# Row maxima of attention scores turned two slots at a time, a turned context kept in memory, routing in groups of six over three rounds

## The reference

```python
x = x + L0_xattn(ctx, ctx, layernorm(x))       # A: one head; keys and values from ctx
x = x + L0_ffn(layernorm(x))                   # B: 32 heads of width 8, then a GELU FFN, one expert a batch
x = x + L1_xattn(layernorm(x), ctx)            # C: one head over ctx, and a self score per token
x = x + L1_ffn(layernorm(x))                   # D: 16 heads of width 16, then a routed FFN
```

## Time and profile before

| | us |
|---|---|
| three timed runs | 2184.40, 2190.86, 2193.01 (median 2190.86) |
| the profiled execution | 2177.86 |
| its span in the profile | 2175.9 |
| TensorE, VectorE, ScalarE, GpSimd busy | 1970.9, 1389.9, 1040.9, 588.0 |

### The profile page before, as it was taken

One profiled execution on the slowest core, in us unless ns is written; L12 is line 12 of the kernel. 1 busy time (PEld: TensorE's weight loads), 2 busy tenths in 40 slices (PEclk: granted clock), 3 DMA queues, 4 the chain that ended last, 5 costly groups with the idle time before them and its releaser, 6 DMA issues. The chain is left out here.

```text
span 2175.9 us, 38554 instructions
## 1 busy us (share of the span) xinstructions
PE 1970.9 (91%) x13917; PEld 1466.8 (67%) x13917; DVE 1389.9 (64%) x3655; ACT 1040.9 (48%) x2001; POOL 588.0 (27%) x476
## 2 busy tenths in 40 slices
PE   4689999999999999999999999999977649999996
PEld 3456666676766666666767666666655428999996
DVE  2336666666766667666766667666677546767663
ACT  1244655565665555565665555564632214333331
POOL 1102031312213121212213131211200136667773
PEclk9679999999999999999999999999988769999998
DMA  5221433514142332414142342414120243344232
GB/s 176 78 73 53 144 112 98 170 67 155 57 146 80 127 129 100 159 58 155 61 145 87 117 144 100 151 42 151 56 69 1 78 144 98 84 123 88 44 53 25
DMA packets 197003, 217.45 MB, mean 100 GB/s; under 512 B 13656, under 2 KB 186544, under 8 KB 196816
## 3 DMA queue, kind: packets, MB, share of 16 engines
q1 hardware_dynamic: 182432, 198.01, 27.4%
q0 software_dynamic: 14384, 16.99, 4.8%
HBM read 146.63 MB, written 68.32 MB: 99 GB/s over the span
## 5 line engine op out<-in xcount | busy, mean ns | idle before, releaser
L1170 DVE TENSOR_REDUCE MX<-bank 128x2 f32<-128x512 f32 x768 | 493.0, 683 | 212.2 <-PE bank L826 211.0
L1408 ACT ACTIVATE PT<-bank 128x512 f32<-128x512 f32 x768 | 416.7, 596 | 233.4 <-PE bank L863 231.6
L826 PE MATMUL bank<-KS,QS 32*128 32x256 f32 (+1 forms) x1536 | 199.4, 338 | 34.9 <-DVE MX L1170 30.0
L878 PE MATMUL bank<-PT,VA 128*32 128x256 f32 x3072 | 213.9, 398 | 7.7 <-ACT PT L1408 5.7
L863 PE MATMUL bank<-QM,KS 32*128 32x256 f32 (+1 forms) x1536 | 193.4, 330 | 13.3 <-ACT PT L1408 12.0
L826 PEld LDWEIGHTS bank<-KS,QS 32*128 32x128 f32 (+1 forms) x1536 | 118.5, 191 | 120.9 <-issue 69.2
L1759 ACT ACTIVATE hid<-bank,b1T 128x512 f32<-128x512 f32 x128 | 87.8, 686 | 228.0 <-PE bank L1711 202.2
L863 PEld LDWEIGHTS bank<-QM,KS 32*128 32x128 f32 (+1 forms) x1536 | 118.8, 189 | 111.0 <-issue 83.3
L678 POOL TENSOR_TENSOR rrB<-uwB,cst 128x4 f32<-128x4 f32 x16 | 16.3, 1018 | 568.6 <-DVE uwB L1145 568.6
L1420 ACT ACTIVATE OS<-bank 128x256 f32<-128x256 f32 x192 | 73.8, 384 | 146.0 <-PE bank L878 144.8
L1724 PE MATMUL bank<-W2h,hTh 128*128 128x256 f32 x512 | 142.8, 279 | 0.0
(11 more groups left out here) (325 smaller groups left out, 3981.8 us busy)
## 6 DMA issues: line engine op xcount, KB each, us to landing
W<-in_L_ffn_w_dram SPq DMA_DIRECT2D x48, 1024.0 KB, 6.9
KS<-k_dram SPq DMA_DIRECT2D x64, 512.0 KB, 5.7
QS<-q_dram SPq DMA_DIRECT2D x64, 512.0 KB, 5.9
k_dram<-qTQ SPq DMA_DIRECT2D x32, 256.0 KB, 2.4
q_dram<-pTQ SPq DMA_DIRECT2D x32, 256.0 KB, 7.1
k_dram<-PRP SPq DMA_DIRECT2D x32, 256.0 KB, 2.4
q_dram<-cTP SPq DMA_DIRECT2D x32, 256.0 KB, 2.5
X<-in_x_dram SPq DMA_DIRECT2D x16, 256.0 KB, 6.2
```

The costliest lines, as they stand in the source:

```text
L826: x = mm(halves(u)[:, r, :], Q[strip, slot, r * P:(r + 1) * P], K[strip, slot, :], start=True, stop=True)
L878: x = mm(bank[4][SLOT * j:SLOT * (j + 1), 0:D], V[:, kc, n * per:n * per + SLOT], PT[:, n % 8, kc, :], start=kc == 0, stop=kc == 1, tile_p ...
L1170: v.tensor_reduce(MX[:, slot % 2, j, :], halves(u), AX, ALU.max, negate=True).then_inc(h.maxed, 1)
L1408: s_.activation(PT[:, n % 8, :, :], halves(2 + n % 2), ACT.Exp, scale=h.scale).then_inc(h.exp, 1)
```

## The change

It has four parts.

1. `maxima`, `turns` and `shifts` work on two slots ("two", eight a full round instead of sixteen). `MT` has one buffer that takes both slots' maxima, in four small operations instead of two a slot; one pair of transposes turns them; one addition of 512 elements shifts both slots' queries. `QM` holds two pairs and `MX` four slots. The spare rows of the stacks hold a pattern of ones that picks the right slot, made at the start by eight VectorE operations in `HT`.
2. SyncE puts A's turned context into memory (`turned`) and gets it back into `cxTP` for C, at step 7 of P. C's own turning on TensorE and copy on ScalarE are gone; step 16 of P is empty.
3. Routing goes in groups of six: (0,6), (6,6) and (12,6), (18,6) in round 15, (24,4) and (28,2) in round 16, none in round 17. `hot` and `spots` are three tiles of A each, so routing waits for A's end and not for the 32-head attention. The first two groups come before D2 of round 15 uses bank 5, the others after it.
4. The orders are new: T has 8 letters instead of 16, and round 15 has an order of its own, `EARLY`, with 29 R; `LATE` has 14 R instead of 29, `LAST` none instead of 7.

```diff
-N_SCORE, N_TURN, N_EXP, N_VALUE, N_LIN2, N_LIN1 = 24, 16, 24, 12, 28, 19
+N_SCORE, N_TURN, N_EXP, N_VALUE, N_LIN2, N_LIN1 = 24, 8, 24, 12, 28, 19
-ROUTED_BY = (((0, 7), (7, 7), (14, 7), (21, 7)), ((28, 2),))
+ROUTED = {-1: (((0, 6), (6, 6)), ((12, 6), (18, 6))), 0: (((24, 4),), ((28, 2),)), 1: ((), ())}
+EARLY = "PPPSRSPTSEERSRSQRPRQTRESVEPRRTSEPQVRQSEPRQPQRQSTPRESSQPREVSPRSTSVRSEPQSEPSPESVETPQSVPQEPSEQTPPSVQSPQSQRPESPEERRQQVEPTQERPREPPRRVRVERRREREVERRPQV"
...
-    round_(n - 1, 1, a=False)
+    round_(n - 1, 1, a=False, order=EARLY)
...
-    link(tt(A[:, 0:2 * n, :], lo.unsqueeze(2).broadcast_to([P, 2 * n, P]), R.iota[:, :].unsqueeze(1).broadcast_to([P, 2 * n, P]), ALU.is_equal))
+        link(tt(A[k // 4][:, 0:m, :], lo[:, k:k + m].unsqueeze(2).broadcast_to([P, m, P]), R.iota[:, :].unsqueeze(1).broadcast_to([P, m, P]), ALU.is_equal))
...
-        QM = sb("QM", [P, 2, D], F32R)
-        MX, MT = sb("MX", [P, 2, 4, 2]), {w: sb(f"MT{w}", [P, 2, 2, P]) for w in (8, 16)}
+        QM = sb("QM", [P, 2, 2, D], F32R)
+        MX, MT = sb("MX", [P, 4, 4, 2]), {w: sb(f"MT{w}", [P, 2, P]) for w in (8, 16)}
...
@@ block.sync, lin1 @@
-                yield from idle(3)
+                yield from idle(2)
+                if a_:
+                    made(act, "A", b, "cxT")
+                    sp.dma_start(turned_d[now(sp, b)], cxTQ[:, :, :]).then_inc(s_cxput, 16)
+                yield
@@ block.sync, lin2 @@
-                yield from idle(15)
+                yield from idle(6)
+                for c in range(DC):
+                    if not first(b):
+                        ready(s_parts[16, "q", c], b * PARTED)
+                ready(s_cxput, b * 16 + 16)
+                sp.dma_start(cxTP[:, :, :], turned_d[now(sp, b)]).then_inc(s_cxget, 16)
+                yield
+                yield from idle(8)
@@ block.tensor, turns @@
-                base = now(t, b * h.slots)
-                for slot in range(h.slots):
-                    t.wait_ge(h.parted, base + (slot + 1))
+                base = now(t, b * h.twos)
+                for two in range(h.twos):
+                    t.wait_ge(h.parted, base + (two + 1))
                     bank4_free(shared)
...
@@ block.tensor, exps @@
-                    if p == 0:
-                        t.wait_ge(h.shifted, base["slot"] + (slot + 1))
+                    if (slot % 2, p) == (0, 0):
+                        t.wait_ge(h.shifted, base["two"] + (slot // 2 + 1))
@@ block.tensor, lin2 @@
-                t.wait_ge(s_cxC, b * 16 + 16)
-                turn(6, CXC).then_inc(*E.tick("cxT"))
                 yield
...
+                t.wait_ge(s_cxget, b * 16 + 16)
                 product(6, qTP, cxTP).then_inc(*E.tick("s"))
@@ block.vector, maxima @@
+                    two = slot // 2
+                    if (slot % 2, p) == (0, 0):
+                        if two >= 2:
+                            v.wait_ge(h.parted, base["two"] + (two - 1))
+                        elif prev:
+                            v.wait_ge(prev[0].parted, prev[1] * prev[0].twos + prev[0].twos - 1 + two)
...
-                    if p == h.pairs - 1:
...
+                    if (slot % 2, p) == (1, h.pairs - 1):
+                        low = MX[:, slot % 4 - 1:slot % 4 + 1, 0:h.nh, :].rearrange("p y j r -> p r j y")
...
+                        if not (first(b) and two == 0):
+                            v.wait_ge(h.turned, base["two"] + two)
+                        for r in range(2):
+                            x = v.tensor_copy(parts[:, r, :, 0:4:2].bitcast(F32R), low[:, r])
+                        x.then_inc(h.negated, 1)
+                        v.wait_ge(h.negated, base["two"] + (two + 1))
+                        for r in range(2):
+                            x = v.tensor_tensor(parts[:, r, :, 1:4:2], low[:, r], parts[:, r, :, 0:4:2], ALU.subtract)
+                        x.then_inc(h.parted, 1)
@@ block.vector, shifts @@
-                    v.tensor_tensor(QM[:, slot % 2, :], QS[h.width][:, slot, :].bitcast(F32), bank[4][:, D:2 * D], ALU.add).then_inc(h.shifted, 1)
+                    v.tensor_tensor(QM[:, two % 2, :, :], QS[h.width][:, 2 * two:2 * two + 2, :].bitcast(F32),
+                                    bank[4][:, D:2 * D].unsqueeze(1).broadcast_to([P, 2, D]), ALU.add).then_inc(h.shifted, 1)
@@ block.vector, routing @@
-                if r == B:
-                    v.wait_ge(h0.st, B * h0.heads)
+                if r == B - 1:
+                    wait(v, pool, "A", B - 1, "xb")
+                    wait(v, dve, "A", B - 1, "x")
...
@@ block.scalar, lin1 @@
+                    if not first(b):
+                        s_.wait_ge(s_cxput, b * 16)
                     take("A", 5, cxTQ, b, "cxT")
@@ block.scalar, lin2 @@
-                yield from idle(4)
-                take("C", 6, cxTP, b, "cxT")
-                yield
+                yield from idle(5)
                 take("C", 7, nTP, b, "nT")
```

150 lines of the change are left out of this document (88 added, 62 removed).

## The result

The change is a gain, and half of what was forecast. Four executions of the kernel after have their median at 2148.65 us (2144.83 to 2156.19), four of the kernel before at 2187.63 (2184.07 to 2193.01): ratio 0.983, 95% interval 0.981 to 0.9855. The forecast was 2112. The profiled execution took 2144.83 us, its span is 2143.0, against 2175.9 before.

What follows compares the result with a forecast made beforehand. TensorE's time was taken to bound full rounds, VectorE's order and the chain through it rounds 16 and 17. Full rounds -45.5, rounds 0 and 1 -3, rounds 15 to 17 -30: 2190.9 - 78.5 = 2112 us, range 2085 to 2140.

Steps and rivals of the forecast that it cites:

- Full rounds: Rounds 2 to 14, 97.3 us each, counted by TensorE's time: 3.5 us less each, -45.5 together (bounds -26 and -65).
- I take 0.37: TensorE time in us of one turn (two transposes); eight turns fewer make 3.0 us a full round (bounds 2.2 and 3.3).
- The context: C's four context transposes leave TensorE: 0.6 us a full round, with the waits for the two new DMAs costing nothing.
- Rival 2: Turns on TensorE cost their weight loads, not their columns: full rounds give 2.4 us each, 2127 us; chance 0.08.
- Round 15: Takes in four routing groups, VectorE becomes its bound: from 94.3 to 112 us, +18 (bounds +9 and +30).
- with 8% of waits: Step for round 15: VectorE's 103 us of work, with 8% of waits added, make 112 us.
- Rival 1: Round 15 jams and gains what round 16 loses, so the tail (rounds 15 to 17) gives 0: 2142 us; chance 0.18.
- the prediction's own signs: Among others: round 15 over 105 us, VectorE over 85% busy there; wrong if rounds 15 to 17 stay above 297.6.
- Round 16: Routing no longer stands before the chain on VectorE: from 128.6 to 82 us, -46 (bounds -57 and -24).
- Round 17: Its routing goes, and pairs of slots take some of the gain back: -2 us (bounds -6 and +3).
- The start: Eight small VectorE operations make the ones at the kernel's start: 0 us, at most +2.
- Rival 3: Exponent products wait for the pair in full rounds, 1.2 us uncovered each: +125 us, 2237 us; chance 0.04.

Runs made afterwards that it cites:

- ctx_back: Kernel after with C's context turned on TensorE and copied by ScalarE again, no put or get: 2147.1 us, full rounds 95.3 us.
- no_onehot15: Kernel after without VectorE's 24 one-hot operations in round 15, TensorE's products kept (those tiles not routed): 2142.6 us, round 15 137.9 us.
- no_routing15: Kernel after with the four routing groups of round 15 left out, order EARLY kept: 2120.0 us, round 15 117.2 us.
- order15: Kernel after with round 15 in the order of the full rounds and its 29 R spread into it: 2150.8 us, round 15 142.4 us.
- vector_alone15: Kernel after without TensorE's routing products and their waits in round 15, VectorE's and ScalarE's steps kept: 2139.4 us, round 15 134.1 us.
- three_two: Kernel after with three routing groups in round 15, in the full rounds' order, and three in round 16, everything computed: 2140.0 us, ratio to before 0.980.
- no_routing: Kernel after without routing of the first thirty tiles, round 15 in the full rounds' order: 2094.8 us, rounds 15 to 17 250.2 us.
- old_order: Kernel after with full rounds in the order of before, every second turn dropped, exponent and value steps put off as needed: 2570.2 us, ratio to before 1.176.
- start_late: Kernel after with the first R of EARLY moved from letter 5 to letter 11: 2145.1 us, round 15 141.3 us.
- onehot_gpsimd: Kernel after with half of the one-hot operations moved from VectorE to GpSimd in rounds 15 and 16: 2156.4 us, ratio to before 0.987.

## Why the prediction was right and wrong

**Full rounds: the sign and the mechanism right, the size off.** -45.5 forecast, -33.6 measured. TensorE's busy time fell to 90.9 a round, close to the forecast; the term that was mis-sized is "I take 0.37" for a turn. ctx_back leaves 0.26 us for each. That is near the shortest distance from start to start, 0.27, which the prediction had read and passed over for a busy figure; but it is a net figure. Busy time fell by 3.2 us a round, less than the single products were busy (8 x 0.41 + 0.66 = 3.9), since they overlap others. The round fell by 2.6, since the holes grew by 0.6, where the sum left them as they were. None of TensorE's waits in the full rounds of after is for a shifted query; over the thirteen rounds those ahead of the exponent products for ScalarE grew from 5.0 to 16.5 us, and those for a maximum from 10.1 to 15.8. Whether the pairs or the new order made them wasn't tried apart. The context gave 0.5 of the forecast 0.6, with no wait of TensorE on the get.

The Trainium skill (Trainium Kernel Development and Optimization, section Performance Expectations) says that matmul busy time misjudges the distance to TensorE's limit and weight loads measure it better. Here the truth lay between the two: busy 3.2 us a round less, weight loads 1.7 less (865.9 to 844.3 over thirteen), the round 2.6. Rival 2, which put 2.4 on it, had the better number for this term.

**Round 15: the step that failed.** The sums were nearly right: VectorE 103 forecast and 109.1 measured (4 us of it are four operations that waited for GpSimd, last section), TensorE 95 and 109.3, of which part is the clock and 3.8 the products for the ranks (lines 235 and 236), which the sum left out. What failed is "with 8% of waits, as little as a queue in fixed order leaves, 112 us". No row showed the 8%. VectorE waits in 24% of the 143.0 us, and TensorE in about as much. The rows for this were on the table: in the earlier trace rows VectorE is busy 90.1 of 128.6 us in round 16, 30% of waits in the one stretch that had routing beside its chain. With 30%, 103 us give 147, near the 143.0, but a share of VectorE's waits is no mechanism: no_onehot15 took 16.5 us off VectorE's sum and the round lost 5.1. The sum also put the new order EARLY at nothing, and no_routing15 takes 117.2 us in it without any routing in the round, already more than the forecast 112. That is no more than a part of it, since order15, in the order of the full rounds, takes 142.4 as well.

The step that failed is to take VectorE's sum as the round's bound and its free time as room. It is not room but the other half of a handshake: each of its steps makes TensorE late, TensorE's next product then makes it late, and routing's own chain through TensorE (ranks, then one-hots, then table) waits in both queues besides. vector_alone15 and no_onehot15 are the evidence that it isn't one sum, three_two and order15 that the last group in a round costs two to four times the one before it.

**Rival 1 is what happened**, and by its own mechanism: "TensorE waits in it, and every row with low TensorE share has a low clock". It said tail 0 and 2142; the tail is +5 and the time 2149, outside the forecast's own range (2085 to 2140) and inside the wider one only because that took in this rival. Its 0.18 was set low by the argument against it ("most routing steps stand at the end of that order, where few products are left"), which holds little: in the order of the full rounds a second group there costs 21 us, and in EARLY the two late groups cost 13.8 (129.2 to 143.0), no less than the two early ones (12.0). The Trainium skill (TensorE: Matmul & The Clock Gate, section HAM oscillation) says that idle holes between bursts bring the clock down, and the trace agrees: 0.96 in round 15 before, with TensorE busy 84.5 of 94.3 us, and 0.79 after, with 109.3 of 143.0. Of the prediction's own signs, round 15 above 105 us came, VectorE above 85% busy did not (76%), and one that it named for being wrong came: rounds 15 to 17 did not fall below 297.6 us but rose to 302.8.

**Round 16** was forecast at 82 and took 86.0, clock 0.84; no_routing shows 82.0 for its floor. The reading that VectorE's routing stood in front of the chain there was right. **Round 17** gave 0.9 for 2, which is within what it wanders (72.0 to 75.0 us in the kernels that have no routing in it). **The start** can't be told from its spread. **Rival 3** is no danger in the kernel as it is, and a large one in another order (old_order).

Not settled: how much of the 48 us of round 15 each cause has. At order15, TensorE's products of routing, the slower clock and the waits come to 25 us of busy time and 22 of idle time more than in no_routing, and what part of either the clock has wasn't tried apart. What the late groups pay for standing behind D2's use of bank 5 wasn't either. And only five orders were tried with four groups in round 15 (EARLY, those of start_late and order15, two with finer steps): a better one isn't ruled out.

## What to carry to other kernels

Before work is moved into an engine's idle time, ask what ends each of its waits: time between two handshakes with the engine that sets the pace is not room, and the waiting share of the most similar loaded stretch was a better price here (30% for 24% measured) than a few per cent. Spread such work over several stages and look at the last portion in each: the group that filled a stage cost 21 us, the one before it 5 to 9, though the first two of round 15 cost 21 together. A new order of steps has a price of its own: try it without the work that it is made for. For small matmuls that go, the shortest distance from start to start in a dense stretch (0.27 us) was nearer here to what the round gave back (0.26 a pair) than their busy time (0.41); it is one case, and growing holes are in it.

## What the runs showed of the hardware

DMAs of one size took two or three times as long where they stood close behind others. DMA issues of the kernel after (KB each, median us to landing):

```profile
k_dram<-qTQ SPq DMA_DIRECT2D x32, 256.0 KB, 2.5
q_dram<-pTQ SPq DMA_DIRECT2D x32, 256.0 KB, 7.3
...
X<-in_x_dram SPq DMA_DIRECT2D x16, 256.0 KB, 6.5
...
CXC<-in_ctx_dram SPq DMA_DIRECT2D x16, 256.0 KB, 2.7
turned_dram<-cxTQ SPq DMA_DIRECT2D x16, 256.0 KB, 6.5
...
cxTP<-turned_dram SPq DMA_DIRECT2D x16, 256.0 KB, 6.5
```

The put and the get of the turned context took 6.5 us where the prediction took the 2.6 of the context's load. It isn't the direction: the load of x takes as long (6.2 us in the kernel before already), and of two puts of 256 KB by the same part, its keys and its queries, one takes 2.5 and one 7.3. What differs is what stands ahead in SyncE's queue. From 697.83 to 704.52 us it issues four loads of keys and queries, and the put, the load of x and the get follow at 705.75, 706.38 and 706.98; the context's load stands alone, at 730.01. The put of the keys at 777.91 has none of them just ahead, that of the queries at 788.53 has four (785.17 to 787.70). That they are the cause wasn't tried apart. The lead of some nine steps hid the 6.5 us.

VectorE and GpSimd hold each other up. Two stretches show it, the first in onehot_gpsimd, the second in the kernel after (start us, us):

```profile
1487.33 1.51 POOL L268 TENSOR_TENSOR pTQ<-XBA 128x512 f32<-128x512 f32 x1
1487.95 1.44 DVE L348 TENSOR_TENSOR NQ<-X,r_iota 128x512 f32<-128x512 f32 x1
1488.81 1.51 POOL L268 TENSOR_TENSOR cTQ<-XBA 128x512 f32<-128x512 f32 x1
1489.42 1.44 DVE L348 TENSOR_TENSOR cxTQ<-X,r_iota 128x512 f32<-128x512 f32 x1
```

```profile
1564.45 1.26 POOL L775 TENSOR_TENSOR YB<-X,rowboD 128x512 f32<-128x512 f32 x1
1564.58 1.17 DVE L310 COPY X<-r_rank 128x6 f32<-128x6 f32 x1
1565.68 1.27 POOL L754 TENSOR_TENSOR XBP<-X,B 128x512 f32<-128x512 f32 x1
1565.78 1.19 DVE L311 TENSOR_SCALAR X<-r_rank 128x6 f32<-128x6 f32 x1
```

In the first, each operation starts while the other engine's still runs, and ends 0.55 us (VectorE) or 0.93 us (GpSimd) after that one's end: one works while the other stands. Three of the four groups of round 15 ran so: the VectorE compares took 0.93 to 1.61 us, and in the one group without GpSimd beside it 0.68 to 0.69. In the second, a copy of six elements a partition, 0.17 us elsewhere, lasts 1.17 us and ends 0.04 us after GpSimd's addition, and so with the next, 0.02 us after; two operations at line 1405 took 1.36 and 1.30 us beside additions, for 0.27 in the full rounds. So the kernel after pays this too, 4 us of VectorE's time in round 15. The maxima and shifts, with an input in PSUM, stayed at 684 and 681 ns; one shift ran wholly beside a GpSimd product (1486.38) in 0.69 us. The Trainium skill (SBUF — State Buffer, section SBUF: two separate sides) has a rule for it: the two engines share a pair of ports as an exclusive lock, and a VectorE operation with two SBUF inputs waits for a GpSimd operation that reads SBUF. The first stretch agrees with that by these numbers; the operations of the second have one input in SBUF, and waited all the same. The experiment that wanted a helper for VectorE had overlooked it.
